# Writing the gate-up product of a mixture-of-experts stage over its PSUM bank instead of into an SBUF buffer

## What is computed

```python
shared = silu(x @ sg_w.T) * (x @ su_w.T) @ sd_w.T
...
comb = jnp.zeros((T, E), x.dtype).at[jnp.arange(T)[:, None], topk_i].add(topk_w)
h = jax.nn.silu(jnp.einsum('th,eih->eti', x, eg_w)) * jnp.einsum('th,eih->eti', x, eu_w)
routed = jnp.einsum('eti,ehi,te->th', h, ed_w, comb)
```

## Time and profile before

| | |
|---|---|
| span of the profiled execution | 1330.2 us |
| its own whole time | not given apart from the span |
| three executions, median | 1331.89 us (1329.06 to 1332.82) |
| TensorE busy | 1123.7 us, 84% |
| VectorE busy | 1048.8 us, 79% |
| ScalarE busy | 723.0 us, 54% |
| GpSimd busy | 457.3 us, 34% |
| expert stage M1, first gate matmul to last residual addition | 550.7 to about 821 us |
| expert stage M2, the same | 1057.4 to about 1326 us |
| mean granted TensorE clock | 0.919 of 2.4 GHz |

### The profile page before, as it was taken

How to read it: one execution, slowest core, us unless ns; L and a number is a source line. 1 busy time by engine, 2 the same in 40 slices (tenths; PEclk the granted TensorE clock), 3 DMA queues, 4 the chain that set the end, 5 groups by cost and what they waited for, 6 DMA issues and landing times. The chain is left out here.

```text
span 1330.2 us, 21650 instructions
## 1 busy us (share of the span) xinstructions
PE 1123.7 (84%) x6256; PEld 494.3 (37%) x6296; DVE 1048.8 (79%) x1763; ACT 723.0 (54%) x1103; POOL 457.3 (34%) x345
## 2 busy tenths in 40 slices
PE   1499999799999955489999996588886299999997
PEld 0212323223223215234444443355556144444443
DVE  8598888688888877778888887564437778888887
ACT  0404676566767843356666664434453166666665
POOL 8300000000000121257677766001100267767775
PEclk9757999999999978699999998788898599999999
DMA  2551101101100380176666761643300077677664
GB/s 57 114 137 26 24 3 26 27 1 25 26 2 1 122 248 19 43 160 165 163 151 163 169 154 39 135 58 47 44 11 19 0 182 161 150 167 163 156 156 101
DMA packets 49932, 120.12 MB, mean 90 GB/s; under 512 B 8377, under 2 KB 34873, under 8 KB 40137
## 3 DMA queue, kind: packets, MB, share of 16 engines
q1 hardware_dynamic: 49864, 119.27, 39.5%
HBM read 103.94 MB, written 14.91 MB: 89 GB/s over the span
## 5 line engine op out<-in xcount | busy, mean ns | idle before, releaser
L489 DVE TENSOR_REDUCE Aatt_mx<-Aatt_sc 128x1 f32<-128x512 f32 x512 | 318.1, 686 | 52.9 <-PE Aatt_sc L367 48.1
L451 ACT ACTIVATE Aatt_prob<-Aatt_st 128x1024 f32<-128x1024 f32 x256 | 248.3, 1021 | 107.1 <-PE Aatt_st L376 106.8
L1407 POOL TENSOR_TENSOR M2ex_low<-M2ex_hid,M2ex_high 128x512 f16<-128x512 f32 x132 | 181.3, 1391 | 92.4 <-ACT M2ex_high L1339 90.6
L1407 POOL TENSOR_TENSOR M1ex_low<-M1ex_hid,M1ex_high 128x512 f16<-128x512 f32 x132 | 180.1, 1381 | 95.7 <-ACT M1ex_high L1339 92.4
L367 PE MATMUL Aatt_sc<-ks,qs 128*128 128x512 bf16 x490 | 187.8, 417 | 21.1 <-issue 8.3
L376 PE MATMUL Aatt_st<-qs,ks 128*128 128x512 bf16 x494 | 149.2, 384 | 2.5 <-ACT Aatt_prob L451 0.7
L1378 DVE TENSOR_TENSOR M1ex_hid<-M1ex_act_up,M1ex_cb 128x512 f32<-128x512 f32 x132 | 139.3, 1056 | 5.2 <-DMA M1ex_cb<-comb 5.2
L1378 DVE TENSOR_TENSOR M2ex_hid<-M2ex_act_up,M2ex_cb 128x512 f32<-128x512 f32 x132 | 138.2, 1048 | 3.9 <-DMA M2ex_cb<-comb 3.9
L387 PE MATMUL Aatt_pv<-Aatt_prob,vg 128*32 128x512 f32 x1024 | 136.4, 605 | 1.5 <-ACT Aatt_prob L451 0.7
L1369 DVE SCALAR_TENSOR_TENSOR M2ex_act_up<-M2ex_up,unscale,M2ex_sil 128x512 f32<-128x512 f32 x132 | 98.5, 746 | 36.2 <-ACT M2ex_sil L1334 32.4
L1369 DVE SCALAR_TENSOR_TENSOR M1ex_act_up<-M1ex_up,unscale,M1ex_sil 128x512 f32<-128x512 f32 x132 | 98.5, 746 | 35.9 <-ACT M1ex_sil L1334 33.1
(11 more groups left out here) (277 smaller groups left out, 1962.1 us busy)
## 6 DMA issues: line engine op xcount, KB each, us to landing
M1ex_cb<-comb SPq DMA_DIRECT2D x64, 512.0 KB, 6.5
M2ex_cb<-comb SPq DMA_DIRECT2D x64, 512.0 KB, 6.4
M_wt<-wsplit SPq DMA_DIRECT2D x66, 192.0 KB
wsplit<-split_cut SPq DMA_DIRECT2D x9, 704.0 KB, 6.5
split_raw<-in_wg_dram SPq DMA_DIRECT2D x6, 704.0 KB, 8.0
stack<-Aqkv_part SPq DMA_DIRECT2D x16, 192.0 KB, 4.2
qs<-stack SPq DMA_DIRECT2D x16, 192.0 KB
ks<-stack SPq DMA_DIRECT2D x16, 192.0 KB
```

The lines of the kernel that those rows point to most:

```text
L451: act.activation(prob[e % 4][:, :, :].rearrange("p a c -> p (a c)"), st[pr][:, :, :].rearrange("p a c -> p (a c)"), ACT.Exp, scale=SCALE). ...
L489: dve.tensor_reduce(mx[k][:, i // 2, i % 2:i % 2 + 1], sc_bank(k, i)[:, :], AX.X, ALU.max).then_inc(red_done, 1)
L1407: pool.tensor_tensor(low[i % 3][:, :], hid[i % 3][:, :], high[i % 3][:, :], ALU.subtract).then_inc(low_ready, 1)
```

## The change

The result of `times_up` is written over the up bank that it has read, and `times_weight` reads it from there. The SBUF buffers `act_up` fall away. Since the bank is now in use until `times_weight` has read it, TensorE waits ahead of the first up matmul of step q until `times_weight` of step q-2 is done (`hid_ready` starts at `ONE` = 1, and `times_weight` of step j brings it to j+2). Its wait ahead of the gate matmuls stays. Lines of the changed file are shifted by one at most.

```diff
-        act_up = [sb(f"act_up{i}", [P, CH], F32) for i in range(3)]
@@ gate_up @@
                 for bank, a, done in ((gate, 0, g_done), (up, 2, u_done)):
                     o = bank[i % 2][:, :]
+                    if bank is up and i >= 2:
+                        pe.wait_ge(hid_ready, ONE + q - 1)
                     pe.matmul(o, wt[k][:, a, :], env.xh[:, cs], start=True, stop=False)
@@ times_up @@
-                dve.scalar_tensor_tensor(act_up[i % 3][:, :], up[i % 2][:, :], env.unscale[:, 1:2], sil[i % 2][:, :],
+                dve.scalar_tensor_tensor(up[i % 2][:, :], up[i % 2][:, :], env.unscale[:, 1:2], sil[i % 2][:, :],
                                          ALU.mult, ALU.mult).then_inc(up_ready, 1)
@@ times_weight @@
-                dve.tensor_tensor(hid[i % 3][:, :], act_up[i % 3][:, :], cb[k][:, c * CH:(c + 1) * CH],
+                dve.tensor_tensor(hid[i % 3][:, :], up[i % 2][:, :], cb[k][:, c * CH:(c + 1) * CH],
                                   ALU.mult).then_inc(hid_ready, 1)
```

## The result

The changed kernel takes 1433.8 us in the median of 4 runs (1431.48 to 1435.78), against 1330.47 us (1325.21 to 1332.82, also 4) before: 1.0788 times as long, with a 95% interval of 1.0754 to 1.0822. That is +103 us. The profiled execution took 1431.48 us and spans 1429.1.

What follows compares the result with a forecast made beforehand. TensorE's issue was taken to bound the kernel at 1.94 us per chunk. A 2.38 us cycle adds 55.5 + 57.2 over two stages, ends -1.4, starts +3: +114 on 1331.89, so 1446 us, range 1408 to 1500.

Steps and rivals of the forecast that it cites:

- The bound before: In the expert stages before the change, TensorE's own issue sets the pace: nine matmuls per chunk, 1.94 us.
- The ring: Cycle up(j), times_up(j), times_weight(j-1), up(j+1), closed by TensorE's new wait: 2.38 us a turn against 1.94.
- 0.43, 0.38, 0.13, 0.66, 0.68 and 0.10: Microseconds: up start to third, its run, handover to times_up, times_up to times_weight starts, times_weight's run, handover to TensorE.
- The bounds: Limits of the cycle's period: 2.25 to 2.50 us, the upper stretched to 2.57 for VectorE writing PSUM.
- The multiplication without the long ones: times_weight on VectorE, one operand now in PSUM, is no longer held up by GpSimd: 0.68 us, mean before 1056 ns.
- the forecast of 1.15: GpSimd's subtraction, free of VectorE's lock, should take its minimum of 1.15 us, well inside 2.38.
- The 0.07: Allowance in us for VectorE writing its result to PSUM, which no row showed; it stretches the period's upper limit to 2.57.
- The start of a stage: TensorE stops at up(6) for routing weights longer than 3.51 us, then one period at 1.2 GHz: +1.5 us per stage.
- The end of a stage: GpSimd has no backlog and ends 4.4 us after the last up matmul instead of 5.2: about -0.7 per stage.
- The wait was not met early: Rival: TensorE's new wait is met in time, it stays back to back, time 1330.5 or 1327 us; chance 0.04.
- the clock held at 1.00: Rival: TensorE's clock gives way to 1.2 GHz in its idle gaps; 1628 us with half the chunks so; chance 0.06.
- that second rival: VectorE in PSUM is slower than allowed or still held up by GpSimd: 1539 or 1579 us; chance 0.10.

## Why the prediction was right

- **The bound before.** TensorE back to back at 1.94 was right: cut below it, the ring no longer shows, and the time ends at 1332.6.
- **The ring.** Right in kind and nearly in size: 2.361 for 2.38. Term by term 0.43, 0.38, 0.13, 0.66, 0.68 and 0.10 were forecast and 0.44, 0.38, 0.14, 0.66, 0.68 and 0.06 measured. The last was the one that I had put between 0.06 and 0.14; a TensorE that has stood 0.4 us is back in 0.06. Of 250 steps this is 5 us of the 12 by which 1446 was too high. TensorE's idle time in front of up, 0.2 to 0.3 us in 126 steps by the forecast, is 0.22 to 0.25 in the rows above and comes 129 times in a stage. The bounds were summed up 0.01 too high: with 0.75 and 0.14 the terms give 2.49, and with the allowance 2.56.
- **The multiplication without the long ones.** Right: at most 692 ns, with the subtraction running into it in nearly every step. For GpSimd the forecast of 1.15 was right but not its reason, that the operand in PSUM frees the subtraction: with the wait alone and both operands in SBUF it takes 1153 to 1161 too. The 0.07 that I allowed for writing PSUM came out at 0.009 on `times_up`, and none of it lies between the starts of the two instructions, 0.66 as before. By an estimate from the fixed 58 and 120 cycles of the Trainium skill ("VectorE: DVE Perf Modes", the section on the TRN2 errata) it should have been 65 ns more for the operand in PSUM; the runs show 680 against 681.
- **The start of a stage.** Wrong in detail, the part of the sum that failed. I let TensorE stand longer than before at the first routing weights and fall to 1.2 GHz, +1.5 us per stage. It stood 1.86 us instead of 3.51, and in M2 2.2 us, much as before (2.14). The ring had already made steps 4 and 5 late, so that the multiplication of step 4 waited 1.51 us for its weights where it had waited 5.24. The clock stayed up. The weights also came sooner after the stage's first matmul: in M1 566.70 - 550.02 = 16.7 us, where it had been 569.10 - 550.74 = 18.4, and in M2 1120.05 - 1103.10 = 16.9, where it had been 1075.38 - 1057.47 = 17.9. In M1 the load itself was quicker, 7.3 us from issue to use instead of 8.9; in M2 it took as long as before, and was issued about 1 us sooner. Why is open. The clock and the weights together are about 6 us of the excess.
- **The end of a stage.** Right: GpSimd is done 4.5 us after the last up matmul's end (863.40 to 867.93), where it was 5.2, for the forecast's -0.7.
- **The sum by stages.** From the first gate to the last up M1 takes 862.57 - 550.02 = 312.6 us, before 261.1; M2 takes 312.9, before 259.0. That is +105 with -1.4 for the ends, 104, and the medians say 103. The rest of the program is unchanged within what differs from one execution to the next: from the last up of M1 to the first gate of M2 it is 240.5 us in this trace, 245.6 in the one before, and 239.7 to 246.2 in all the traces kept. That is why the two profiled spans differ by 98.9 and not by 103.
- **The rivals.** The wait was not met early; the clock held at 1.00 with TensorE short of a start for 0.40 us in every 2.36; and VectorE in PSUM was not slower by more than 9 ns. The run with the wait alone shows what that second rival would have cost, 1496, had the operand stayed in SBUF.

## What to carry to other kernels

Before an intermediate is put where the next matmul wants to write, follow the new wait round through each engine's program order: from the producer's end through everything that stands ahead of the releasing instruction, back to the producer. If that circle is longer than the period that the bound engine keeps, the kernel takes the circle's period, whatever the shares of busy time say (here 2.59, 2.36 and 2.10 us for three lengths of it, and TensorE's own 1.94 once it was shorter than that). The second bank gave no slack here, because VectorE's order puts `times_up` of the next step ahead of the multiplication that frees the bank. Either turn the consumer's order so that the release comes before the next step's work, or leave the copy in SBUF: work taken off an engine that does not bind pays for nothing.

## What the runs showed of the hardware

- VectorE writing its result over its own operand in PSUM, 128x512 float32 with a pointer scalar, takes 759 ns against 751 to SBUF, with a spread of 3 ns; multiplying from PSUM and SBUF takes 680 against 681 from SBUF alone, where GpSimd is out of the way. I had expected some cost.
- Moving one operand from SBUF to PSUM frees VectorE's multiplication of GpSimd's subtraction. With the wait alone, two operands in SBUF, it began during a subtraction in 129 of the 132 steps of M1, ended 0.55 us behind it each time, and took up to 1580 ns. In the changed kernel it began during a subtraction in 129 steps as well, and never took more than 692.
- GpSimd's subtraction is drawn out where VectorE's multiplication began ahead of it or with it. In M1 of the kernel before, the 76 subtractions that began during a multiplication, or at most 10 ns ahead of one, took 1488 ns or more, and the other 56 at most 1162. With the wait alone it always begins first, and takes 1153 to 1161 although the multiplication has both operands in SBUF. In the changed kernel too it always begins first, so its 1152 to 1160 there do not show that the operand in PSUM frees it.
- TensorE stops of 0.40 us in every 2.36 left the granted clock at 1.00 from up(6) to up(131) of both stages, 295 us each. So did the single stops of 1.86 and 2.2 us ahead of them, where 3.51 us in the kernel before were followed by 0.72.
